# One-hot rows shared with ScalarE, and another order of the sums on TensorE, in a DLRM tower kernel

## What is computed

```python
e = jnp.stack([tbl_f[ids[:, f]] for f in range(40)], axis=1)      # 512, 40, 64
viW = jnp.einsum('bpd,pde->bpe', e[:, i_idx, :], W)               # 780 pairs
z = jnp.einsum('bpe,bpe->bp', viW, e[:, j_idx, :])
h = jnp.concatenate([z, dense_ctx], axis=1)
h = jnp.maximum(h @ W_top1 + b_top1, 0.0)                         # 796 -> 512
h = jnp.maximum(h @ W_top2 + b_top2, 0.0)                         # 512 -> 256
y = h @ W_top3                                                    # 256 -> 1
```

## Time and profile before

| | |
|---|---|
| median of 3 runs | 317.81 us (317.76 to 318.22) |
| the profiled execution's own time | 317.81 us |
| its span | 316.0 us |
| PE busy | 309.4 us, 98% of the span |
| DVE busy | 256.4 us, 81% |
| POOL busy | 196.5 us, 62% |
| ACT busy | 115.0 us, 36% |
| granted TensorE clock | 1.00 throughout |

### The profile page before, as it was taken

One profiled execution on the slowest core, in us unless ns is written; L12 is line 12 of the kernel. 1 busy time (PEld: TensorE's weight loads), 2 busy tenths in 40 slices (PEclk: granted clock), 3 DMA queues, 4 the chain that ended last, 5 costly groups with the idle time before them and its releaser, 6 DMA issues.

```text
span 316.0 us, 4373 instructions
## 1 busy us (share of the span) xinstructions
PE 309.4 (98%) x1684; PEld 112.6 (36%) x1684; DVE 256.4 (81%) x264; ACT 115.0 (36%) x296; POOL 196.5 (62%) x156
## 2 busy tenths in 40 slices
PE   6999999999999999999999999999999999999996
PEld 2444223332333333332333333333333333333364
DVE  4995998688998989999898899999999999940000
ACT  0203830644545954689984511075000000001032
POOL 3798777777777777777755778845666555550000
DMA  6981333323223662323228569887777666420000
GB/s 150 326 271 21 70 84 81 76 59 89 65 64 90 242 209 64 92 58 82 75 64 161 142 143 206 154 188 168 166 164 162 133 134 135 91 41 8 12 0 0
DMA packets 16188, 35.86 MB, mean 113 GB/s; under 512 B 3748, under 2 KB 4776, under 8 KB 14504
## 3 DMA queue, kind: packets, MB, share of 16 engines
q0 software_dynamic: 5824, 16.79, 27.7%
q1 hardware_dynamic: 7848, 13.96, 14.9%
q10 hardware_dynamic: 2496, 4.84, 4.4%
HBM read 22.86 MB, written 0.00 MB: 72 GB/s over the span
## 4 chain that ended last, share of the span: by engine, by line
PE 89%; DVE 5%; DMA 3%; issue 1%; ACT 0%; ACTq 0%; DVEq 0%
PE y_ps L636 54%; PE z_ps L660 22%; PE y_ps L670 5%; DMA prod<-in_tbl 2%; DVE prod L529 2%; PE t_ps L670 2%; PE y_ps L717 2%; PE t_ps L542 2%; DMA prod<-hot_ids 1%; DVE x L452 1%; DVE x_quad L458 1%; DVE zT L462 1%; PE y_ps L542 1%; DVE prod L452 1%; PE t_ps L717 1%
## 5 line engine op out<-in xcount | busy, mean ns | idle before, releaser
L636 PE MATMUL y_ps<-x,w 64*128 64x512 f32 x780 | 184.2, 606 | 0.9 <-DVE prod L529 0.6
L322 POOL DMA_INDIRECT gathered<-in_tbl,ids_sb x128 | 130.9, 1023 | 43.2 <-issue 38.7
L529 DVE TENSOR_TENSOR prod<-y_ps,x 128x1024 f32<-128x1024 f32 x89 | 103.5, 1211 | 15.3 <-PE y_ps L636 13.7
L529 DVE TENSOR_TENSOR prod<-y_ps,x_quad 128x1024 f32<-128x1024 f32 x96 | 110.5, 1215 | 2.7 <-PE y_ps L636 2.4
L636 PEld LDWEIGHTS y_ps<-x,w 64*128 64x128 f32 x780 | 69.7, 186 | 114.1 <-issue 79.5
L385 ACT COPY x<-x_fold 32x128 f32<-32x128 f32 x208 | 61.5, 295 | 66.9 <-DVE x_fold L497 64.7
L347 POOL TENSOR_TENSOR prod<-prod 128x2048 f32<-128x2048 f32 x12 | 54.5, 4544 | 33.8 <-DVE prod L529 33.8
L660 PE MATMUL z_ps<-prod,select 128*32 128x512 f32 x588 | 73.4, 600 | 0.0
L660 PEld LDWEIGHTS z_ps<-prod,select 128*32 128x32 f32 x588 | 14.3, 108 | 52.0 <-issue 38.3
L414 ACT COPY zT<-z_ps 128x512 f32<-128x512 f32 x6 | 3.5, 585 | 67.1 <-PE z_ps L660 67.0
L408 ACT COPY x_mix<-x 64x512 f32<-64x512 f32 x40 | 24.7, 617 | 0.7
(11 more groups left out here) (47 smaller groups left out, 82.0 us busy)
## 6 DMA issues: line engine op xcount, KB each, us to landing
w<-w_rows SPq DMA_DIRECT2D x48, 256.0 KB, 3.0
prod<-prod POOLq DMA_DIRECT2D x12, 1024.0 KB, 7.7
gathered<-in_tbl,ids_sb POOLq DMA_INDIRECT x128, 2.6
w<-w_rows ACTq DMA_DIRECT2D x1, 1792.0 KB
prod<-in_tbl ACTq DMA_DIRECT2D x6, 256.0 KB, 6.5
prod<-hot_ids SPq DMA_DIRECT2D x4, 256.0 KB, 6.5
prod<-in_tbl ACTq DMA_DIRECT2D x4, 128.0 KB, 3.1
w<-w_rows ACTq DMA_DIRECT2D x1, 512.0 KB
```

Of the source, the lines that this page charges most:

```text
L322: nc.gpsimd.indirect_dma_start(gathered[:, slot, c, s * DIM:(s + 1) * DIM], None, tables[f][:, :], bass.IndirectOffsetOnAxis(ap=ids_sb[:, ...
L529: nc.vector.tensor_tensor(prod[:, d % PROD_SLOTS, :, :], y_ps[:, d % DUO_SLOTS, :, :], factor, ALU.mult).then_inc(prod_ready, 1)
L636: last = nc.tensor.matmul(y_ps[:, d % DUO_SLOTS, half, :], w[rows, r % W_SLOTS, d % ROUND, :], x[rows, units[half], :], start=True, stop=True)
```

## The change

Three things change. (1) ScalarE makes eight of the 32 one-hot rows: q = 5, 6, 7 of units 1 and 2, and q = 6, 7 of unit 3 (`MADE_BY_ACT`). It computes Abs(id - number) and then Relu(1 - that), two ACTIVATEs per row, the second behind a wait for the first (`hot_apart`), and TensorE waits for such a row on `hot_made`. Unit 1's rows stand ahead of every copy of x; unit u + 2's rows stand behind the copy of unit u. (2) The sum of round r - 1 stands behind the matmuls of round r up to r = 24, and that of r - 3 from r = 27 on. The first sum also waits for the copy of unit 4, which leaves the bank that the sums use. The copies of z move with the sums. (3) Behind rounds 25 and 26 there is no sum but one matmul of layer 1 each (blocks 0 and 1, m = 0), and these two leave the tail.

```diff
+EARLY_LAG = 1
 LAG = 3
+LAYER1_AT = [25, 26]
+MADE_BY_ACT = {1: (5, 6, 7), 2: (5, 6, 7), 3: (6, 7)}
...
+    def sums_at(self, r):
+
+        if r < LAYER1_AT[0]:
+            return r - EARLY_LAG if r >= EARLY_LAG else None
+        return None if r in LAYER1_AT else r - LAG
...
+            def make_one_hot(u):
+
+                act.wait_ge(lane_rows_loaded, 16)
+                act.wait_ge(hot_ids_loaded[u], 16)
+                before = sum(len(MADE_BY_ACT[v]) for v in MADE_BY_ACT if v < u)
+                for n, q in enumerate(MADE_BY_ACT[u]):
+                    rows = hot[per_lane * u + q]
+                    nc.scalar.activation(rows, hot_ids_sb[u], ACT.Abs,
+                                         bias=lane_rows_sb[:, per_lane + q:per_lane + q + 1]).then_inc(hot_apart, 1)
+                    act.wait_ge(hot_apart, before + n + 1)
+                    nc.scalar.activation(rows, rows, ACT.Relu, bias=1.0, scale=-1.0).then_inc(hot_made, 1)
+
             def save_x(u):
                 if u < HOT_UNITS:
                     act.wait_ge(hot_picked, u + 1)
                     nc.scalar.copy(x[:, u, :], hot_ps[u]).then_inc(x_ready, 1)
+                    if u + 2 in MADE_BY_ACT:
+                        make_one_hot(u + 2)
...
+            make_one_hot(1)
             for r in range(len(plan.rounds)):
...
-                if (r - LAG) % BLOCK_ROUNDS == BLOCK_ROUNDS - 1 and r >= LAG:
-                    save_z((r - LAG) // BLOCK_ROUNDS)
+                summed_round = plan.sums_at(r)
+                if summed_round is not None and summed_round % BLOCK_ROUNDS == BLOCK_ROUNDS - 1:
+                    save_z(summed_round // BLOCK_ROUNDS)
...
-                one_hot(u, every[early:])
+                one_hot(u, [q for q in every[early:] if q not in MADE_BY_ACT[u]])
...
                     if q >= early:
-                        pe.wait_ge(hot_ready, per_lane * u + q + 1)
+                        if q in MADE_BY_ACT[u]:
+                            pe.wait_ge(hot_made, made_ahead + MADE_BY_ACT[u].index(q) + 1)
+                        else:
+                            pe.wait_ge(hot_ready, per_lane * u - made_ahead + q + 1)
                         pick_rows(u, q, 0)
                     pick_rows(u, q, 1)
...
-                if r == LAG:
+                if r == EARLY_LAG:
                     pe.wait_ge(select_loaded, 16)
-                if r >= LAG:
-                    sum_round(r - LAG)
-
-            pe.wait_ge(w1_loaded, 32)
-            full = list(range(NBLK - 1))
+
+                    pe.wait_ge(x_ready, HOT_UNITS + 1)
+                if r in LAYER1_AT:
+
+                    n = LAYER1_AT.index(r)
+                    pe.wait_ge(w1_loaded, 32)
+                    pe.wait_ge(z_saved, n + 1)
+                    layer1(0, full[n:n + 1], first=n == 0)
+                elif plan.sums_at(r) is not None:
+                    sum_round(plan.sums_at(r))
+
             pe.wait_ge(z_saved, NBLK - 2)
-            layer1(0, full[:-1], first=True)
+            layer1(0, full[len(LAYER1_AT):-1])
```

More of the change, by code:

```diff
@@ L183, in dlrm_tower @@
         select = sb("select", [ROWS, 2, 2 * QUAD])
-        per_lane = lane_rows.shape[1]
-        lane_rows_sb = sb("lane_rows_sb", [LANES, per_lane])
+        per_lane = lane_rows.shape[1] // 2
+        lane_rows_sb = sb("lane_rows_sb", [LANES, 2 * per_lane])
         gathered = sb("gathered", [ROWS, GATHER_SLOTS, CHUNKS, 2 * DIM])
@@ L244, in dlrm_tower @@
         hot_ready = sem("hot_ready")
+        hot_apart = sem("hot_apart")
+        hot_made = sem("hot_made")
         rest_ready = sem("rest_ready")
@@ L579, in pick_unit @@
                 early = 3 if u == 1 else 0
+                made_ahead = sum(len(MADE_BY_ACT[v]) for v in MADE_BY_ACT if v < u)
                 pe.wait_ge(hot_tables_loaded[u], 32)
@@ L672, in layer1 @@
                 return done
+            full = list(range(NBLK - 1))
             warm_up()
@@ L795 @@
     lane_rows = np.arange(LANES * per_lane, dtype=np.float32).reshape(LANES, -1)
+    lane_rows = np.concatenate([lane_rows, -lane_rows], axis=1)
     hot_ids = np.ascontiguousarray(np.asarray(inputs["ids"])[:, HOT_FIELDS].T).view(np.int16)[:, ::2]
```

## The result

Before 318.0 us (median of 4, 317.76 to 318.22), after **322.0 us** (median of 4, 321.77 to 322.07): ratio 1.0123, 95% interval 1.011 to 1.0137. The interval lies clear of 1: the change makes the kernel slower, 0.7 us less so than forecast. The profiled execution of the changed kernel took 322.07 us, with a span of 320.3 us against 316.0.

What follows compares the result with a forecast made beforehand. TensorE was taken as the bound, busy 309.4 of 316.0 us, with holes only between 29.5 and 47.8 us. Terms 6.0 - 2.15 + 0.55 + 0.5 = +4.9 us on 317.81 us gave 322.7 us, range 320.7 to 325.0 us.

Steps and rivals of the forecast that it cites:

- The sum: Whole kernel: 6.0 - 2.15 + 0.55 + 0.5 = +4.9 us on 317.81 us, forecast 322.7 us.
- The head: Everything before the first duo: ScalarE's rows at 2.27 us each come late, unit 2 ends 6.0 us later.
- Six rows: Units 1 and 2 on ScalarE: unit 2's end is 15.9 us + six rows, 29.5 us instead of 23.50.
- The holes: TensorE's gaps before the first sum: sums one round behind fill them, 3.23 - 1.07 = 2.15 us gained.
- Rival C: Early sums delay VectorE's products (three buffers only): gain 1.0 us instead of 2.15, 323.9 us; chance 0.12 together with Rival D.
- The z copy: Round 9: the copy stands behind unit 9's copies in ScalarE's queue, so TensorE's next sum waits 0.55 us.
- Rounds 25 and on: Lone layer 1 blocks and VectorE's fold transposes use up its slack, small waits appear: 0.5 us lost.
- Rival A: ScalarE's one-hot rows are cheap on 16-bit data: no change at 317.8 us, or 316.0 us; chance 0.08.
- Rival B: TensorE's clock falls to 1.2 GHz in waits for late rows in units 1 and 2: 325.7 us; chance 0.10.
- unit 1 alone hit: Smaller form of Rival B: lower clock in unit 1 only costs 0.3 us, since ScalarE is waited for anyway.
- I would be wrong if the clock dips: Sign against the forecast: a dip of TensorE's granted clock in the changed profile; no size given.
- Rival D: Head's price right, but W's loads start 6.8 us later and meet the gathers: top of range; chance 0.12 together with Rival C.

Runs made afterwards that it cites:

- version 2: Changed kernel with ScalarE's eight rows kept, but all sums three rounds behind and layer 1 wholly in the tail: 322.88 us, ratio 1.0151.
- version 4: Changed kernel, but ScalarE keeps unit 1's three rows only; VectorE makes those of units 2 and 3: 321.93 us, ratio 1.0095.
- experiment 3: Changed kernel, but unit 1's three rows are VectorE's again; ScalarE keeps five rows, of units 2 and 3: 316.95 us, ratio 0.9953.
- experiment 5: version 4 with six matmuls on zeros, whose result is unused, ahead of q6 and q7 of unit 1: 320.6 us, ratio 1.0093.
- Experiment 1: Changed kernel, but VectorE makes all 32 one-hot rows again; new sum order and two layer 1 blocks stay: 317.09 us, ratio 0.9966.
- Experiment 7: Kernel of experiment 3 with no layer 1 matmul behind rounds 25 and 26, all layer 1 blocks in the tail: 318.72 us, ratio 1.0034.

## Why the prediction was right

**The sum.** The measured terms give 4.86 - 1.83 + 0.53 + 0.69 = 4.25 us, forecast 4.9. Each term has the forecast's sign and place. That the total is only 0.65 us off is in part luck: the head was put 1.14 us too high, the others together 0.49 us too low.

**The head: right in mechanism, 1.1 us too dear.** It said 6.0 us and measured 4.86. The error lies in two inputs. The row was put at 2.27 us and took 2.13 (Abs 1.14, Relu 1.06, 0.03 us for the hand-over, less 0.10 us of overlap with the next row): six rows, 0.84 us. The table load began at 11.46 instead of 11.75 us in this execution: 0.29 us. (It varies from run to run: the same queue has 11.56 us in version 2 and 11.77 in version 4.) The Trainium skill (ScalarE: Activation LUTs, "What ACT_TABLE_LOAD costs") states 280 ns + 0.833 ns per element with a pointer bias. For Abs that is an estimate of 1133 ns, and the trace agrees with 1140 ns. The prediction took the pointer price for Relu too, whose bias is a constant; the trace has 1057 ns. The same section states that back-to-back ACTIVATEs overlap by about 93 ns; the trace shows 0.10 us between two rows, none between a row's Abs and the Relu that waits for it, and the prediction had left it out. Experiment 2 shows the term by itself, experiment 3 that a row costs nothing where it is not late.

**The chain's account was incomplete.** "Six rows" gives unit 2's end only if units 1 and 2 both hang on ScalarE. Experiments 4 and 5 show that unit 1's three rows alone make 3.65 of the 5.2 us between the first duos of versions 1 and 2 at the full clock, since their lateness can't be made up, and more where the clock falls. The end of the chain was right, but the six rows have no equal shares in it.

**The holes: 1.83 us gained, forecast 2.15.** The same sum gives 20.20 - 14.5 - 0.6 - 3.7 = 1.4 us that are no work of the duos after the change, not 1.07. TensorE was full from the first sum on, as predicted: no row shows it waiting from there to round 9. The 0.3 us are in two readings. The first eight duos take 8.43 us up to the sum (34.34 to 42.77), not 8.3: the eighth, alone ahead of another kind of matmul, takes 1.05 us, not 0.93. And the round with the transpose takes 4.42 us (50.12 to 54.54), not 3.63 + 0.6. **Rival C** (three buffers too few) did not happen, since no sum delayed a product for which TensorE then waited. Experiment 1 confirms the gain.

**The z copy: 0.53 us, forecast 0.55**, and in round 9, where it was looked for.

**Rounds 25 and on: 0.69 us, forecast 0.5**, of which the lone blocks are 0.39. Experiment 7 shows that the blocks fill waits.

**Rival A** (cheap rows) fell at once: (1140 - 685 - 30) / 512 is again 0.83 ns per element, on 16-bit data. (The rival's "half the price per row" is a slip: half of 2.27 us is 1.14, while its times follow from the 1.42 us that it names.) **Rival B** came true in its condition but not in its price. The clock fell behind two waits of 1.50 us. The Trainium skill (TensorE: Matmul & The Clock Gate, "HAM oscillation") describes a kernel whose clock drops in its waits for DMA, which it gives as some 3 to 5 us; here half of that was enough in some executions and not in others. The fall cost the changed kernel nothing, because ScalarE's chain was longer (experiment 2); the prediction had put this case, unit 1 alone hit, at 0.3 us. The sentence that I would be wrong if the clock dips was itself wrong: a dip costs only where TensorE sets the pace, as in experiment 4. **Rival D** did not happen: W's loads started at 19.74 us instead of 13.66, and no duo waited for them.

## What to carry to other kernels

A helper engine's share of a job is free only up to the moment at which each piece is needed. So lay its ready times beside the consumer's need times, piece by piece: here five rows are free, and three more, the first ones, cost 3.3 us at the full clock and 4.8 us in the median. When the producer of a value moves earlier, look at what stands ahead of its consumer in every in-order queue; one copy behind a transpose of the next round cost 0.53 us in one schedule and 7 us in another. Work that nothing waits for is worth most where its engine would wait for another: two lone matmul blocks were worth 1.8 us where VectorE sets the pace.

## What the runs showed that I had not expected

The clock's fall is no fixed property of a program. The changed kernel and version 2 have the same head with the same two waits of 1.50 us. One was granted 0.72 in the stretch from 18 to 24 us, the other 1.00. In version 4, whose waits are 0.49, 1.50 and 1.26 us, it was 0.50, and its runs spread over 2.8 us (320.26 to 323.06), while those of the changed kernel, where the dip is covered, spread over 0.3 us. Rarely it fell in the kernel before too (one run of 18 on one chip, 320.41 us at 0.995). What decides whether it falls, and for how long, was not found.
